# A fused conditioning and LoRA feed-forward kernel: two tiles as a 2x2 block product with seven block products

## The reference, cut to what matters

```python
# x: (32, 64, 1024); cond_128: (32, 128)
h = gelu(cond @ W0 + b0); h = gelu(h @ W1 + b1)
att = softmax(h @ W2 + b2)                          # (32, 8)
agg_w = einsum('bk,koi->boi', att, weight)          # a 64x64 matrix for each of 32 samples
agg_b = att @ bias_k
u = einsum('boi,bih->boh', agg_w, x) + agg_b[:, :, None]
xf = u.reshape(-1, 1024)
probs = softmax(xf @ gate_W.T); w, sel = top_k(probs, 2); w = w / w.sum()
lora = (xf @ A.T) * (dense(w, sel) * 2.0)           # 8 experts x rank 8
out = x + xf @ W_base.T + lora @ B
```

## Time and profile before

| what | value |
|---|---|
| median of 3 runs (lowest, highest) | 267.11 us (266.07, 269.69) |
| span of the profiled execution | 265.7 us |
| median less that span | 1.4 us |
| PE, DVE, ACT, POOL busy | 96%, 53%, 26%, 25% |
| time of one tile in the loop | 14.64 us |

### The profile page before, as it was taken

The page is one execution under the profiler, slowest core; times in us unless marked ns, Lnnn a source line. Parts: engine busy times, 40 slices in busy tenths (PEclk is TensorE's granted clock), DMA queues, the critical chain, the costliest instruction groups (busy, mean ns, idle before and its releaser), DMA issues.

```text
span 265.7 us, 4272 instructions
## 1 busy us (share of the span) xinstructions
PE 254.0 (96%) x1451; PEld 247.9 (93%) x1451; DVE 141.1 (53%) x398; ACT 69.0 (26%) x156; POOL 65.2 (25%) x46
## 2 busy tenths in 40 slices
PE   8699679999999999999999999999999999999994
...
DMA packets 9527, 31.02 MB, mean 117 GB/s; under 512 B 1072, under 2 KB 1584, under 8 KB 9520
## 3 DMA queue, kind: packets, MB, share of 16 engines
q1 hardware_dynamic: 9520, 30.93, 33.3%
...
## 4 chain that ended last, share of the span: by engine, by line
PE 85%; DVE 9%; DMA 2%; ACT 2%; SPq 1%; issue 1%; DVEq 0%; ACTq 0%
PE z_ps L660 23%; PE z_ps L662 23%; PE z_ps L661 23%; PE o_ps L679 3%; DVE w_lo L455 3%; PE o_ps L690 3%; PE o_ps L688 3%; PE o_ps L676 3%; PE o_ps L674 3%; DMA w_raw<-wext_in 2%; DVE b_lo L607 1%; ACT w_hi L335 1%; DVE blk_lo L467 1%; DVE gate L509 1%; DVE lora_split L517 1%; DVE att_rep L569 1%
## 5 line engine op out<-in xcount | busy, mean ns | idle before, releaser
L660 PE MATMUL z_ps<-w_hi,xt_hi 128*128 128x366 f32 (+1 forms) x384 | 130.8, 341 | 4.1 <-DVE w_lo L455 4.0
L662 PE MATMUL z_ps<-w_hi,xt_lo 128*128 128x366 f32 (+1 forms) x384 | 129.1, 336 | 0.0
L661 PE MATMUL z_ps<-w_lo,xt_hi 128*128 128x366 f32 (+1 forms) x384 | 128.9, 336 | 0.0
L660 PEld LDWEIGHTS z_ps<-w_hi,xt_hi 128*128 128x128 f32 x384 | 74.4, 194 | 6.0 <-DVE w_lo L455 5.0
L460 DVE TENSOR_TENSOR z_lo<-z_ps,z_hi 128x366 fp32r<-128x366 f32 (+1 forms) x48 | 25.8, 538 | 96.4 <-ACT z_hi L341 96.3
L296 POOL TENSOR_TENSOR xt_lo<-xt_raw,xt_hi 128x1024 fp32r<-128x1024 f32 x14 | 36.8, 2628 | 154.3 <-ACT xt_hi L331 154.3
L661 PEld LDWEIGHTS z_ps<-w_lo,xt_hi 128*128 128x128 f32 x384 | 74.6, 194 | 0.0
L662 PEld LDWEIGHTS z_ps<-w_hi,xt_lo 128*128 128x128 f32 x384 | 74.2, 193 | 0.0
L341 ACT ACTIVATE z_hi<-z_ps 128x366 fp32r<-128x366 f32 (+1 forms) x48 | 22.8, 475 | 149.9 <-PE z_ps L662 149.8
L476 DVE SCALAR_TENSOR_TENSOR x_nat<-w_sum,bias,x_nat 128x1024 f32<-128x1024 f32 (+2 forms) x18 | 23.0, 1280 | 3.8 <-DMA x_nat<-x_in 3.8
L531 DVE TENSOR_TENSOR out_sb<-o_ps,x_nat 128x366 f32<-128x366 f32 (+1 forms) x44 | 19.9, 505 | 4.7 <-PE o_ps L690 3.8
...
## 6 DMA issues: line engine op xcount, KB each, us to landing
x_nat<-x_in SPq DMA_DIRECT2D x16, 512.0 KB, 4.6
xt_raw<-xt_in SPq DMA_DIRECT2D x15, 512.0 KB, 5.1
out<-out_sb SPq DMA_DIRECT2D x15, 512.0 KB, 3.0
...
```

Source lines behind the costliest of these rows:

```text
L660: nc.tensor.matmul(dst, hi, w_cols(w_hi, g, k), start=(k == 0), stop=False)
L661: nc.tensor.matmul(dst, hi, w_cols(w_lo, g, k), start=False, stop=False)
L662: last = nc.tensor.matmul(dst, lo, w_cols(w_hi, g, k), start=False, stop=(k == KC - 1))
```

## The change

Two tiles are multiplied together. Their rows and features form a 2x2 block matrix: A11 and A12 are the first and second 512 features of the even tile, A21 and A22 those of the odd one (each 128 rows). W is cut into feature halves and column halves, B11, B12, B21, B22; each column half is again two quarters of 274 columns, s = 0 ("low half" of a step) and s = 1 ("high half"). For each s the products, in PE's order (`sub`), are

- P1 = A11 B11, P2 = A22 T4, P3 = S2 T2, P4 = A12 B21, P5 = S3 T3, P6 = S1 T1, P7 = S4 B22,
- with S1 = A21 + A22, S2 = S1 - A11, S3 = A11 - A21, S4 = A12 - S2 for every pair (POOL, `operands`) and T1 = B12 - B11, T2 = B22 - T1, T3 = B22 - B12, T4 = B21 - T2 once at the start (`t_first` on POOL, `t_second` on DVE), all split again into hi and lo.

P1, P3 and P5 pile up in the bank `x_ps`, P2 goes to `w_ps`, P4 to `z_ps`, P6 and then P7 to `y_ps`. ACT copies `x_ps` to SBUF (`zf`) after P1, P3 and P5 (`copy`), DVE adds: Z11 = P1 + P4, Z21 = (P1+P3+P5) + P2, Z22 = (P1+P3+P5) + P6, Z12 = (P1+P3) + (P6+P7). Each product is 4 chunks of 3 matmuls of 274 columns. `z_high` and `z_low` now read `zf` in SBUF. `gate_mix` and `unit` mix the channels and add the expert part, in eight units for a pair (units 0 and 1 mix in `gate_mix`); one gating serves both tiles; the output is added in place in `x_nat` and stored in 8 pieces for a pair. The first pair is done with the plain eight products for each s. The loads of x come in quarters.

The core of the diff:

```diff
+HALF = D // 2
+HC = KC // 2
...
+CW = NCOL // 4
...
+        UNITS = [(0, 0, 0, Z11, 0), (1, 0, 0, Z21, 1), (1, 1, 0, Z22, 2), (0, 1, 0, Z12, 0),
+                 (0, 0, 1, Z11, 1), (1, 0, 1, Z21, 2), (1, 1, 1, Z22, 0), (0, 1, 1, Z12, 1)]
...
-            with pool.Fori(1, PAIRS) as j:
-                x_low(2 * j, 0)
-                x_low(2 * j + 1, 1)
...
+            def t_first(s):
+                pool.wait_ge(w_lo_ready, 8 * s + 8)
+                pool.wait_ge(fold_step, 6 * s + 6)
+                nc.gpsimd.tensor_tensor(t1[s][:, :], w_raw[B12][s][:, :], w_raw[B11][s][:, :],
+                                        ALU.subtract).then_inc(t13_ready, 1)
+                pool.wait_ge(t13_ready, 2 * s + 1)
+                nc.gpsimd.tensor_tensor(t3[s][:, :], w_raw[B22][s][:, :], w_raw[B12][s][:, :],
+                                        ALU.subtract).then_inc(t13_ready, 1)
...
+            def operands(q, first=False):
+                def a_low(slot, r, n, high):
+                    pool.wait_ge(op_hi_ready, op_high_count(q, high + 1))
+                    nc.gpsimd.tensor_tensor(op_lo[:, slot, :], xt_raw[:, r, :], op_hi[:, slot, :].bitcast(F32),
+                                            ALU.subtract).then_inc(a_lo_ready, 1)
+                pool.wait_ge(xr_loaded[R21], 16 * (q + 1))
+                pool.wait_ge(xr_loaded[R22], 16 * (q + 1))
+                if not first:
+                    pool.wait_ge(s_lo_ready, s_low_count(q - 1, 3))
+                nc.gpsimd.tensor_tensor(s1_raw[:, :], xt_raw[:, R21, :], xt_raw[:, R22, :],
+                                        ALU.add).then_inc(s_ready, 1)
+                a_low(O_A11, R11, 1, 0)
+                pool.wait_ge(s_ready, s_count(q, 1))
+                nc.gpsimd.tensor_tensor(xt_raw[:, R21, :], xt_raw[:, R11, :], xt_raw[:, R21, :],
+                                        ALU.subtract).then_inc(s_ready, 1)
+                a_low(O_A22, R22, 2, 1)
+                pool.wait_ge(s_ready, s_count(q, 2))
+                pool.wait_ge(a_lo_ready, a_low_count(q, 1))
+                nc.gpsimd.tensor_tensor(xt_raw[:, R11, :], s1_raw[:, :], xt_raw[:, R11, :],
+                                        ALU.subtract).then_inc(s_ready, 1)
+                a_low(O_A12, R12, 3, 3)
+                pool.wait_ge(s_ready, s_count(q, 3))
+                pool.wait_ge(a_lo_ready, a_low_count(q, 3))
+                nc.gpsimd.tensor_tensor(xt_raw[:, R12, :], xt_raw[:, R12, :], xt_raw[:, R11, :],
+                                        ALU.subtract).then_inc(s_ready, 1)
...
+            t_first(0)
+            operands(1, first=True)
+            t_first(1)
+            with pool.Fori(2, PAIRS) as q:
+                operands(q)
...
+            def step(p, more=True, first=False):
+                if not first:
+                    z_high(p - 1, 1, Z12)
+                s_high(p, O_S1, s1_raw[:, :], 5, 1)
+                s_high(p, O_S4, xt_raw[:, R12, :], 6, 4)
+                copy(p, 0, x_ps, Z11, 1)
+                block_high(p, 1)
+                copy(p, 0, x_ps, Z12, 2)
+                block_high(p, 0)
+                z_high(p, 0, Z11)
+                copy(p, 0, x_ps, U3, 3)
+                z_high(p, 0, Z21)
+                z_high(p, 0, Z22)
+                z_high(p, 0, Z12)
+                ratio_exp(p)
+                copy(p, 1, x_ps, Z11, 1)
+                if more:
+                    raw_high(p + 1, O_A11, R11, 0)
+                    raw_high(p + 1, O_A22, R22, 1)
+                copy(p, 1, x_ps, Z12, 2)
+                if more:
+                    s_high(p + 1, O_S2, xt_raw[:, R11, :], 2, 3)
+                lora_copy(p)
+                z_high(p, 1, Z11)
+                copy(p, 1, x_ps, U3, 3)
+                z_high(p, 1, Z21)
+                if more:
+                    raw_high(p + 1, O_A12, R12, 3)
+                    s_high(p + 1, O_S3, xt_raw[:, R21, :], 4, 2)
+                z_high(p, 1, Z22)
...
+            def t_highs(s):
+                act.wait_ge(t24_ready, 2 * s + 2)
+                t_high(t4_hi[s], t4[s])
+                t_high(t2_hi[s], t2[s])
+                act.wait_ge(t13_ready, 2 * s + 2)
+                act.wait_ge(sum_mm, 2 * s + 2)
+                t_high(t1_hi[s], t1[s])
+                act.wait_ge(t_lo_ready, 4 * s + 3)
+                t_high(t3_hi[s], t3[s])
...
+            def z_add(p, s, kind, bank, other):
+                if kind == Z21:
+                    dve.wait_ge(copied, copies(p, s) + 3)
+                else:
+                    dve.wait_ge(prod_done, products(p, s) + {Z11: 4, Z22: 6, Z12: 7}[kind])
+                if kind in (Z11, Z12):
+                    dve.wait_ge(copied, copies(p, s) + (1 if kind == Z11 else 2))
+                else:
+                    dve.wait_ge(z_lo_ready, z_count(p, s - 1, kind))
+                nc.vector.tensor_tensor(zf[:, kind, :], bank[:, 0:CW], zf[:, other, :],
+                                        ALU.add).then_inc(z_added, 1)
...
+            t_second(0)
+            dve.wait_ge(sum_ready, 4)
+            x_bias(0, 0)
+            add_out(0, 0)
+            add_out(0, 1)
+            z_low(0, 1, Z22, x_ps)
+            add_out(0, 2)
+            t_lows(0)
+            s_low(1, O_S2, xt_raw[:, R11, :])
+            s_low(1, O_S3, xt_raw[:, R21, :])
+            z_low(0, 1, Z12, y_ps)
+            t_second(1)
+            t_lows(1)
+            step(1, first=True)
...
+            def step(p, more=True, first=False):
                 if not first:
+                    z_12(p - 1, 1)
+                add_out(p - 1, 3)
+                add_out(p - 1, 4)
+                s_low(p, O_S1, s1_raw[:, :])
+                s_low(p, O_S4, xt_raw[:, R12, :])
+                add_out(p - 1, 5)
+                add_out(p - 1, 6)
+                block_low(p, 1)
+                add_out(p - 1, 7)
+                block_low(p, 0)
+                for z in (z_11, z_21, z_22, z_12):
+                    z(p, 0)
+                gating(p)
+                z_11(p, 1)
+                z_21(p, 1)
+                x_bias(p, 0)
+                x_bias(p, 1)
+                z_22(p, 1)
+                add_out(p, 0)
+                add_out(p, 1)
+                add_out(p, 2)
+                if more:
+                    s_low(p + 1, O_S2, xt_raw[:, R11, :])
+                    s_low(p + 1, O_S3, xt_raw[:, R21, :])
...
+            def sub(p, s, between, first=False):
+                later = s == 1 or not first
+                pe.wait_ge(a_lo_ready, a_low_count(p, 1))
+                if later:
+                    pe.wait_ge(copied, copies(p, s))
+                else:
+                    pe.wait_ge(z_lo_ready, 7)
+                product(x_ps, O_A11, w_hi[B11][s], w_lo[B11][s], True)
+                between(0)
+                pe.wait_ge(a_lo_ready, a_low_count(p, 2))
+                if later:
+                    pe.wait_ge(z_added, z_added_count(p, s - 1, Z21))
...
+                product(w_ps, O_A22, t4_hi[s], t4_lo[s], True)
+                between(1)
+                pe.wait_ge(s_lo_ready, s_low_count(p, 1))
+                pe.wait_ge(copied, copies(p, s) + 1)
...
+                product(x_ps, O_S2, t2_hi[s], t2_lo[s], False)
+                between(2)
+                pe.wait_ge(a_lo_ready, a_low_count(p, 3))
+                if later:
+                    pe.wait_ge(z_added, z_added_count(p, s - 1, Z11))
+                product(z_ps, O_A12, w_hi[B21][s], w_lo[B21][s], True)
+                between(3)
+                pe.wait_ge(s_lo_ready, s_low_count(p, 2))
+                pe.wait_ge(copied, copies(p, s) + 2)
...
+                product(x_ps, O_S3, t3_hi[s], t3_lo[s], False)
+                between(4)
+                pe.wait_ge(s_lo_ready, s_low_count(p, 3))
+                if later:
+                    pe.wait_ge(z_added, z_added_count(p, s - 1, Z12))
+                else:
+                    pe.wait_ge(z_lo_ready, 8)
+                product(y_ps, O_S1, t1_hi[s], t1_lo[s], True)
+                between(5)
+                pe.wait_ge(s_lo_ready, s_low_count(p, 4))
+                pe.wait_ge(z_added, z_added_count(p, s, Z22))
+                product(y_ps, O_S4, w_hi[B22][s], w_lo[B22][s], False)
+                between(6)
...
+            def step(p, first=False):
+                def between_low(n):
+                    if n < 3:
+                        unit(p - 1, 5 + n)
+                    if n >= 5:
+                        gate_mix(p, n - 5)
+                def between_high(n):
+                    if n == 3:
+                        transpose_lora(p)
+                    if n == 4:
+                        unit(p, 0)
+                    if n == 5:
+                        unit(p, 1)
+                        unit(p, 2)
+                    if n == 6:
+                        unit(p, 3)
+                        unit(p, 4)
+                sub(p, 0, between_low, first)
+                sub(p, 1, between_high, first)
```

993 lines of the change are left out of this document (543 added, 450 removed).

## The result

The changed kernel takes 336.81 us (median of 4 runs, 334.72 to 340.55) against 266.59 for the kernel before: ratio 1.262, 95% interval 1.254 to 1.270. The profiled execution took 334.72, its span is 333.0. The forecast was 316 us, and its range ended at 336.

What follows compares the result with a forecast made beforehand. PE alone bounded the kernel before; afterwards PE would wait on the other engines' chains. Start 94, six pairs of 33.3 and end 21 gave 314.8, plus 1.4 for median over span: 316 us, 18% slower, range 284 to 336.

Steps and rivals of the forecast that it cites:

- the sum: Whole kernel: 94 for the start, 6 x 33.3 for the pairs, 21 for the end, plus 1.4: 316 us.
- end of step 1's low half: End of the start, through P7 of the first step's low half: forecast near 94 us.
- six pairs: The loop: six pairs of tiles at 33.3 us each, against 29.28 a pair before.
- the end: Last high half, from P7 low to the last store, without Wait 3 or POOL work: 21 us.
- also the clock falls: Rival, chance 0.20: PE's clock drops after long waits, 1.5 us a pair and 2 at the start: 327 us.
- PE's own sum: PE's matmuls in a pair at 0.124 us per 274 columns: 26.0 us if nothing waits, against 29.28.
- Wait 1: Low half, before P7: PE waits for Z22's addition, a chain from P5's end; 0.7 us.
- Wait 2: High half, before P7: same chain with both `x_bias` in it, 2.5 us; 3.8 with the port.
- Wait 3: High half, before unit 0: `lora_t` queued on ACT behind S2, which waits for POOL's four operations; 2.3 us.
- Wait 4, the port: DVE operations with both inputs in SBUF and POOL's exclude each other; adds 1.3 to Wait 2, 0.4 to Wait 3.
- The start: DVE's and POOL's work, 78.9 us times 0.92, sets when DVE leaves `t_lows(1)`: 84.5 us.
- The whole gain in the loop is gone before anything else is counted: Loop: PE's 26.0 us plus the fixed waits 0.7 and 2.5 makes 29.2 a pair, the old 29.28.

Runs made afterwards that it cites:

- fill_start_longer: fill_waits with constant matmuls also in three waits of the start, 168 of them in the longest; 325.7 us.
- fill_waits: Changed kernel with constant matmuls in each pair from 1 on, 18 ahead of the transposes and 17 ahead of P7 in the high half; 326.3 us.
- s2_behind_lora: Changed kernel with ACT's rounded S2 moved behind the copy of `lora_t`; 336.1 us.
- pool_after_gating: Changed kernel with POOL's four operations of a pair made to wait until DVE has done the gating; 330.9 us.
- s2_last: Changed kernel with POOL's four operations behind the gating and ACT's rounded S2 behind the rounded Z22, A12 rounded ahead of it; 323.4 us.
- folds_narrow: Changed kernel with the additions of POOL's four folds in the start cut to 274, 16 and 16 columns, output not the reference's; 326.0 us.
- pool_narrow_in_loop: Changed kernel with POOL's seven operations of a pair on 16 of 512 columns from pair 2 on, output not the reference's; 306.9 us.
- x_bias_split: s2_last with the first `x_bias` right behind the gating, POOL's four operations behind that, the second `x_bias` behind the first output addition; 298.8 us.

## Why the prediction was wrong

The direction and most terms held. The forecast was 20.8 us too short, and the measured time lies 0.8 above its range. The step that failed is **the sum, which counts every matmul of the loop and start at full clock**, and leaves the falls to a rival with a chance of 0.20. The runs show 11.1 us for them: fill_start_longer, which only keeps PE active in the waits of loop and start, takes 325.7 in place of 336.8, and that lies inside the range. Piece by piece, from the profiled execution:

| | forecast | measured | of it |
|---|---|---|---|
| end of step 1's low half | 94 | 98.95 | 2.0 clock (fill_start_longer against fill_waits), 1.7 DVE later, 1.3 the chain behind |
| six pairs | 199.8 | 211.2 | 8.7 clock (fill_waits, 6 x 1.45), 2.7 the rest; PE's slower pace alone would be 3.8 |
| the end | 21 | 22.9 | 1.4 clock (14 matmuls at 0.228 from 323.87 on), and the terms of my sum add up to 21.5, not 21 |
| median above span | 1.4 | 3.8 | 1.7 lie outside the span; 2.1 are the other runs, slower at lower mean clocks (0.893, 0.883, 0.874 against 0.903), so perhaps more falls, which no trace shows |

- **The rival "also the clock falls"** was right: forecast 1.5 a pair and 2 in the start, measured 1.45 and 2.0. With it the sum is 327. Part of that is luck: I placed the fall behind Wait 2, and most of them lie behind the wait ahead of the transposes. What spoke against the rival ("no single long wait inside an otherwise dense stretch" shown to bring a fall) was absence of a row, not a row. The other 10 us are spread over the table: 3.0 in the start, 2.7 in the pairs, 1.9 in the end and 2.4 outside the span.
- **PE's own sum**: 0.124 a matmul was short. 274 columns start 0.127 apart (one product: 138.30 to 139.70, eleven steps), 3.8 us in six pairs. The isolated gap of 117 ns in the Trainium skill ("TensorE: Matmul & The Clock Gate", Back-to-back issue gap) does not agree; the row of 292 columns was the nearer guide. PE was to be busy 78% in the loop and is 83%, partly because a matmul at the lower level is longer.
- **Wait 1**: 0.7 forecast, 0.69 to 0.89 measured in the loop.
- **Wait 2**: 3.8 forecast, 2.31 to 3.23 measured. Its two parts are seen apart: 2.23 with POOL's operations narrow (2.5 forecast), and 3.48 for the two `x_bias` where they meet POOL in place of 2.47 in that kernel, so 1.0 for the port where I had 1.3.
- **Wait 3**: right in size (2.3 + 0.4 forecast, 2.45 measured) and wrong in mechanism, so the size was luck. I had the gating stretched by 0.4 and ACT's queue as what ends the wait; the gating was stretched by 4.1 and ended it, and the queue on ACT came free at the same moment (S2 is rounded from 142.34 on, the transposes start at 142.43), unseen. s2_behind_lora and pool_after_gating show each alone, and s2_last both removed.
- **Wait 4, the port**: the exclusion holds, down to operations of 16 elements: L763 took 1.30 beside POOL and 0.18 without. It reaches further than my rule of two inputs in SBUF: the CAST of `lora_split`, which has one, took 1.17 beside POOL and 0.23 without. The Trainium skill's exclusive lock ("SBUF — State Buffer", Who interferes with whom) agrees. What I mis-sized is that each of several small operations in a row can wait for one of POOL's: 4.1 us for four of them, where I had 0.4.
- **The start**: DVE left `t_lows(1)` at 86.2 (84.5 forecast). The number held, its mechanism is not shown: folds_narrow gave 10.0 of the 14.3 us that the sum of both engines' work asks for, and the trace has POOL and DVE waiting for each other in one chain. No run separates the two.
- **"The whole gain in the loop is gone before anything else is counted"**: this held. pool_narrow_in_loop has Waits 1 and 2 and no other of note, and its pairs without a fall take 30.0 us, against the 29.28 of before (29.2 forecast). Where all but 2 us of waits were taken out, the pair still took 29.5. x_bias_split shows what it is made of: the stretch of 29.45 us from 157.50 on is 26.5 of matmuls at their usual distance, 1.5 ahead of unit 4, 0.85 ahead of P7 in the low half, 0.3 ahead of P7 in the high half, and 0.3 of longer first steps behind a wait.
